# A norm shared by two engines, logits read by token from one bank, and the routing cut short

## The reference, cut to what matters

```python
x = layernorm(target)                      # (32, 256, 128): 32 batches, 256 tokens, 128 features
# branch 1: attention, 16 heads of width 8, causal, then proj, + x, layer norm, * gamma + beta
qkv = x @ w_qkv; scores = q @ k.T / sqrt(8); attn = softmax(causal(scores))
a = layernorm((attn @ v) @ w_proj + b_proj + x) * ln_gamma + ln_beta
# branch 2: mixture of 8 experts, each token goes to its 2 best
probs = softmax(x @ Wr.T); topv, topi = top_k(probs, 2)
m = sum_k topv[k] * (gelu(x @ W1[topi[k]] + b1[topi[k]]) @ W2[topi[k]] + b2[topi[k]])
out = target + a + m
```

## Time and profile before

| | |
|---|---|
| median of 3 runs | 861.58 us (860.87 to 865.58) |
| the profiled execution: time, span | 864.38 us, 862.6 us |
| mean granted TensorE clock | 0.94 of full speed |
| busy share of the span: PE, DVE, ACT, POOL | 82%, 81%, 62%, 62% |
| TensorE clock and PE busy in slices 2 to 5 of 40 (22 to 108 us) | 0.5 to 0.9 of full speed; 3 to 7 tenths |
| the chain that ended last: PE, DVE, DMA | 62%, 13%, 7% |

### The profile page before, as it was taken

One profiled execution on the slowest core, in us unless ns is written; L12 is line 12 of the kernel. 1 busy time (PEld: TensorE's weight loads), 2 busy tenths in 40 slices (PEclk: granted clock), 3 DMA queues, 4 the chain that ended last, 5 costly groups with the idle time before them and its releaser, 6 DMA issues.

```text
span 862.6 us, 24985 instructions
## 1 busy us (share of the span) xinstructions
PE 708.1 (82%) x7699; PEld 523.8 (61%) x7700; DVE 701.1 (81%) x1644; ACT 534.9 (62%) x1061; POOL 533.9 (62%) x572
## 2 busy tenths in 40 slices
PE   0463479999999999999999988857999999999900
PEld 0241246666666666666666556536888898888800
DVE  4866877899989989998989988857888888888745
ACT  0472046565667566666666656537989999999800
POOL 4619046767777776767777677533667776667710
PEclk9985779999999999999999999988999999999955
DMA  7922123232323323232324343111332333323189
GB/s 216 398 59 98 43 65 102 84 113 80 108 89 99 105 80 105 81 110 79 119 86 149 107 125 109 51 33 43 86 85 81 87 87 84 85 79 84 56 260 335
DMA packets 107105, 93.66 MB, mean 109 GB/s; under 512 B 16554, under 2 KB 89394, under 8 KB 107060
## 3 DMA queue, kind: packets, MB, share of 16 engines
q1 hardware_dynamic: 89300, 70.26, 26.2%
q0 software_dynamic: 8704, 18.17, 6.5%
q10 hardware_dynamic: 9056, 4.66, 1.8%
HBM read 43.85 MB, written 48.93 MB: 108 GB/s over the span
## 4 chain that ended last, share of the span: by engine, by line
PE 62%; DVE 13%; DMA 7%; issue 6%; SPq 4%; ACT 2%; POOL 2%; DVEq 1%; POOLq 0%; ACTq 0%
PE wide L1243 11%; PE bank_head L1133 7%; PE bank_head L1234 6%; PE bank_maxB L1234 6%; PE wide L1098 5%; PE bank_maxA L1112 4%; PE bank_maxB L1112 4%; DMA xn_rows<-parts_dram 3%; PE bank_misc L1155 3%; DMA k_cat<-qk_rows 3%; DVE shift L903 2%; PE wide L1102 2%; PE bank_maxA L1116 2%; PE bank_maxB L1116 2%; SPq L458 2%
## 5 line engine op out<-in xcount | busy, mean ns | idle before, releaser
L558 POOL TENSOR_SCALAR_AFFINE_SELECT probs<-probs 128x512 f32<-128x512 f32 (+1 forms) x192 | 155.8, 820 | 102.1 <-ACT probs L648 101.7
L648 ACT ACTIVATE probs<-wide 128x1024 f32<-128x1024 f32 x192 | 188.8, 1018 | 42.4 <-PE wide L1102 22.0
L596 POOL DMA_INDIRECT parts_dram<-o_T,dest x144 | 160.3, 1114 | 74.9 <-issue 47.7
L549 POOL DMA_INDIRECT x_slots<-xn_rows,slot_i x128 | 127.1, 993 | 59.0 <-issue 30.0
L903 DVE TENSOR_REDUCE shift<-bank_maxA 128x2 f32<-128x512 f32 (+1 forms) x192 | 132.1, 688 | 18.9 <-PE bank_maxA L1116 12.5
L903 DVE TENSOR_REDUCE shift<-bank_maxB 128x2 f32<-128x512 f32 (+1 forms) x192 | 131.5, 685 | 4.9 <-PE bank_maxB L1116 0.8
L693 ACT ACTIVATE probs<-wide,b_all 128x256 f32<-128x256 f32 x288 | 121.4, 478 | 17.3 <-PE wide L1243 9.5
L1243 PE MATMUL wide<-lgT,xnT_all 128*128 128x256 f16 x864 | 107.9, 275 | 4.3 <-DVE lgT L1014 4.1
L1133 PE MATMUL bank_head<-probs,v_aug 128*32 128x256 f32 (+1 forms) x2048 | 98.1, 332 | 12.8 <-POOL probs L558 12.3
L997 DVE TENSOR_TENSOR probs<-probs 128x512 f16<-128x512 f32 x144 | 99.7, 693 | 5.5 <-ACT probs L699 1.1
L1112 PE MATMUL bank_maxA<-k_cat,q_diag 128*128 128x128 f16 (+1 forms) x512 | 76.2, 252 | 33.1 <-DVE shift L903 18.9
(11 more groups left out here) (174 smaller groups left out, 1293.3 us busy)
## 6 DMA issues: line engine op xcount, KB each, us to landing
qk_rows<-split SPq DMA_DIRECT2D x32, 512.0 KB, 3.2
x_slots<-fill SPq DMA_DIRECT2D x16, 598.5 KB, 7.1
fill<-x_slots SPq DMA_DIRECT2D x72, 133.0 KB
q_diag<-qk_rows SPq DMA_DIRECT2D x256, 32.0 KB
k_cat<-qk_rows SPq DMA_DIRECT2D x64, 128.0 KB
xn_rows<-parts_dram SPq DMA_DIRECT2D x8, 1024.0 KB, 11.8
out<-x_all ACTq DMA_DIRECT2D x8, 512.0 KB, 9.6
parts_dram<-o_T,dest POOLq DMA_INDIRECT x144
```

Source lines behind the costliest of these rows:

```text
L549: pool.indirect_dma_start(out=x_slots, out_offset=bass.IndirectOffsetOnAxis(ap=slot_i[:, t, c:c + 1], axis=0), in_=xn_rows[:, t, :], in_of ...
L558: pool.affine_select(out=part, in_=part, compare_op=ALU.is_ge, fill=0.0, base=0, pattern=[[0, n], [1, P]], channel_multiplier=-1).then_inc ...
L596: pool.indirect_dma_start(out=parts_dram, out_offset=bass.IndirectOffsetOnAxis(ap=dest[:, of, t:t + 1].bitcast(U32), axis=0), in_=y[:, of ...
L648: act.activation(probs[:, u, :], ps[:, :], ACT.Exp, scale=SCALE).then_inc(empty, 1)
```

## The change

- **Norm.** The input comes in eight half chunks. DVE does all statistics first, then also a small `offset` = -mean * rstd for each chunk; ACT normalises groups 0 to 9 itself, straight from the input (`Identity` with scale and bias, four operations a group), DVE groups 10 to 15. Both write `xn_all` directly; `stage`, `stage_T` and their copies are gone, and so are the loops around these groups. PE transposes from `xn_all`, and ACT makes one copy of each PSUM bank, `xnT_all`.
- **Logits.** PE takes the transposed tile as the stationary operand and the router's weights (8 columns) as the moving one, so that logits come out by token, all 64 tiles in one PSUM bank (`wide[0]`). The transposes back and the copies L615, L619 are gone.
- **Clearing.** `q_diag` is cleared in two halves after the first and second power, `v_aug` after the third.
- **Picks.** They compare logits straight from PSUM, without the exponential; the marks are bf16; PE counts both picks by accumulation. 12 operations. The exponential moves to ACT after step 1, the division and the small weights into `places`.
- **Beta.** POOL adds `beta` for one batch in each step, ahead of the power L585, in place of the eight pieces L544. DVE's `last` waits for it in each step.
- **Experts.** `pack_experts` runs after step 3 in place of step 32; `split_b2` in step 33, after `oT1`.

```diff
+        others, place, rank, prob = (probs[:, u, 0:NT * E].rearrange("p (t e) -> p t e", e=E) for u in range(4))
+        is_top16, key16 = (probs[:, 4, NT * E // 2 * u:NT * E // 2 * (u + 1)].bitcast(BF16).rearrange("p (t e) -> p t e", e=E) for u in range(2))
+        pick16 = probs[:, 5, 0:NT * E].bitcast(BF16).rearrange("p (c t e) -> p c t e", c=2, e=E)
...
+        logits = wide[0][:, 0:NT * E].rearrange("p (t e) -> p t e", e=E)
...
-        ROUTE_PICKED = 18
+        ACT_GROUPS = 10
+        ROUTE_PICKED = 11
         EXPERTS_PACKED = 16
-        ROUTE_DONE = 43
...
+        ROUTE_DONE = 38
+        def wait_normed(eng, g):
+            if g < ACT_GROUPS:
+                eng.wait_ge(normed_act, g + 1)
+            else:
+                eng.wait_ge(normed_dve, g - ACT_GROUPS + 1)
...
-            for c in range(CHUNKS):
...
+            for c in range(2 * CHUNKS):
+                cols = slice(c * TC // 2, (c + 1) * TC // 2)
+                sp.dma_start(x_all[:, cols, :], xt[:, cols, :]).then_inc(x_loaded[c], 16)
...
+            sp.wait_ge(consts, 28)
...
-                    pool.memset(q_diag[:, :, :, :, :], 0.0).then_inc(consts, 1)
-                elif c == 1:
+                if c < 2:
+                    pool.memset(q_diag[:, c, :, :, :], 0.0).then_inc(consts, 1)
+                elif c == 2:
                     pool.memset(v_aug[:, :, :, :, :], 0.0).then_inc(consts, 1)
-                    pool.wait_ge(consts, 26)
+                    pool.wait_ge(consts, 27)
                     pool.memset(v_aug[:, :, :, :, HD:HD + 1], 1.0).then_inc(consts, 1)
...
+            wait_normed(pool, ACT_GROUPS - 1)
+            wait_normed(pool, GROUPS - 1)
...
+                    mine = x_all[:, bass.ds(b * QT, QT), :]
+                    pool.tensor_tensor(mine, mine, beta_bc[:, :].rearrange("p (o d) -> p o d", o=1).to_broadcast([P, QT, D]),
+                                       ALU.add).then_inc(offset_ready, 1)
...
+            def copy_group(g):
                 act.wait_ge(xnT_filled, g + 1)
...
+                act.activation(xnT_all[:, g * (4 * P):(g + 1) * (4 * P)], bank[("maxA", "maxB")[g % 2]][:, :], ACT.Copy).then_inc(xnT_ready, 1)
+            for g in range(GROUPS):
+                if g < ACT_GROUPS:
+                    act.wait_ge(moments_ready, g // (GROUPS // CHUNKS) + 1)
+                    for t in range(4 * g, 4 * g + 4):
+                        ins = act.activation(xn_all[:, t, :], x_all[:, t, :], ACT.Identity, bias=offset[:, t:t + 1], scale=rstd[:, t:t + 1])
+                    ins.then_inc(normed_act, 1)
+                if g > 0:
+                    copy_group(g - 1)
+            copy_group(GROUPS - 1)
             def exp_of_logits():
...
+                act.wait_ge(less_top, 2)
+                act.activation(prob[:, :, :], prob[:, :, :], ACT.Exp).then_inc(exp_router, 1)
+                act.activation(top[:, 1, :], top[:, 1, :], ACT.Exp).then_inc(exp_router, 1)
...
+            def normalise_group(g):
+                for t in range(4 * g, 4 * g + 4):
+                    ins = V.tensor_scalar(xn_all[:, t, :], x_all[:, t, :], mean[:, t:t + 1], rstd[:, t:t + 1], ALU.subtract, ALU.mult)
+                ins.then_inc(normed_dve, 1)
+            def offsets(c):
+                cols = slice(c * TC, (c + 1) * TC)
+                dve.wait_ge(rstd_ready, c + 1)
+                V.scalar_tensor_tensor(out=offset[:, cols], in0=mean[:, cols], scalar=-1.0, in1=rstd[:, cols],
+                                       op0=ALU.mult, op1=ALU.mult).then_inc(moments_ready, 1)
             count = 2
...
+            for c in range(CHUNKS):
+                for h in range(2):
+                    dve.wait_ge(x_loaded[2 * c + h], 16)
+                    for t in range(c * TC + h * TC // 2, c * TC + (h + 1) * TC // 2):
+                        V.bn_stats(stats[:, t, :], x_all[:, t, :]).then_inc(prep, 1)
...
+                if c > 0:
+                    offsets(c - 1)
+            offsets(CHUNKS - 1)
+            for g in range(ACT_GROUPS, GROUPS):
+                normalise_group(g)
...
+                then(V.tensor_copy(order16[:, :], order[:, :]))
+                dve.wait_ge(logits_filled, 1)
+                for c in range(2):
+                    of = (logits, others)[c]
+                    then(V.tensor_reduce(top[:, c, :], of[:, :, :], axis=AX.X, op=ALU.max))
+                    then(V.tensor_tensor(is_top16[:, :, :], of[:, :, :], over_experts(top[:, c, :]), ALU.is_equal))
+                    then(V.tensor_tensor(key16[:, :, :], is_top16[:, :, :], over_tiles(order16[:, :], NT), ALU.mult))
+                    then(V.tensor_reduce(best[:, c, :], key16[:, :, :], axis=AX.X, op=ALU.max))
+                    then(V.tensor_tensor(pick16[:, c, :, :], over_tiles(order16[:, :], NT), over_experts(best[:, c, :]), ALU.is_equal))
                     if c == 0:
...
+                        then(V.scalar_tensor_tensor(out=others[:, :, :].rearrange("p t e -> p (t e)"),
+                                                    in0=pick16[:, 0, :, :].rearrange("p t e -> p (t e)"), scalar=-FAR,
+                                                    in1=wide[0][:, 0:NT * E], op0=ALU.mult, op1=ALU.add))
+                assert route_count == ROUTE_PICKED + 1, route_count
             def places():
                 nonlocal route_count
...
+                V.tensor_tensor(prob[:, :, :], logits[:, :, :], over_experts(top[:, 0, :]), ALU.subtract).then_inc(less_top, 1)
+                V.tensor_tensor(top[:, 1, :], top[:, 1, :], top[:, 0, :], ALU.subtract).then_inc(less_top, 1)
+                then(V.tensor_scalar(xn_rows[:, :, D + 4], best[:, 0, :], -1.0, float(E), ALU.mult, ALU.add))
                 dve.wait_ge(route_counts, 1)
...
+                total = wide[1][:, 512:1024]
+                then(V.tensor_reduce(padded[:, :], total.rearrange("p (t e) -> p e t", e=E), axis=AX.X, op=ALU.add))
+                then(V.tensor_scalar(padded_i[:, :], padded[:, :], float(S - 1), None, ALU.add))
                 then(V.tensor_scalar(padded_i[:, :], padded_i[:, :], S.bit_length() - 1, None, ALU.logical_shift_right))
                 then(V.tensor_scalar(padded[:, :], padded_i[:, :], float(S), None, ALU.mult))
                 then(V.tensor_tensor_scan(ends[:, :], ones[:, 0:E], padded[:, :], 0.0, ALU.mult, ALU.add))
                 then(V.tensor_tensor(padded[:, :], ends[:, :], padded[:, :], ALU.subtract))
...
+                for e in range(E):
+                    V.tensor_tensor_scan(place[:, :, e], ones[:, :], total.rearrange("p (t e) -> p t e", e=E)[:, :, e],
+                                         padded[:, e:e + 1], ALU.mult, ALU.add).then_inc(route, 1)
+                    route_count += 1
+                dve.wait_ge(exp_router, 2)
+                then(V.tensor_reduce(red[:, :], prob[:, :, :], axis=AX.X, op=ALU.add))
+                then(V.tensor_tensor(rank[:, :, :], wide[1][:, 0:512].rearrange("p (t e) -> p t e", e=E), place[:, :, :], ALU.add))
                 for c in range(2):
...
+                    V.tensor_tensor((others, place)[c][:, :, :], pick16[:, c, :, :], rank[:, :, :], ALU.mult).then_inc(route, 1)
+                    route_count += 1
+                then(V.reciprocal(xn_rows[:, :, D], red[:, :]))
+                then(V.tensor_tensor(red[:, :], top[:, 1, :], xn_rows[:, :, D], ALU.mult))
+                then(V.tensor_tensor(xn_rows[:, :, D + 2], red[:, :], xn_rows[:, :, D], ALU.subtract))
+                for c in range(2):
+                    V.tensor_reduce(slot[:, c, :], (others, place)[c][:, :, :], axis=AX.X, op=ALU.add).then_inc(route, 1)
+                    route_count += 1
+                for c in range(2):
+                    dve.wait_ge(route, route_count - 1)
                     then(V.tensor_copy(slot_i[:, :, c], slot[:, c, :]))
...
+                        if what == "oT1" and isinstance(s, int) and s == B + 1:
+                            split_b2()
...
-                if isinstance(s, int) and s == B:
-                    split_b2()
+                if isinstance(s, int) and s == FINISH:
                     pack_experts()
...
+            def router(g):
+                pe.wait_ge(xnT_ready, g + 1)
+                for t in range(4 * g, 4 * g + 4):
+                    last = M(logits[:, t, :], xnT_all[:, P * t:P * (t + 1)], wrT[:, 0:E], start=True, stop=True, skip_group_check=True)
+                if g == GROUPS - 1:
+                    last.then_inc(logits_filled, 1)
...
+            for g in range(GROUPS):
+                wait_normed(pe, g)
+                if g > 1:
+                    pe.wait_ge(xnT_ready, g - 1)
+                ps = bank[("maxA", "maxB")[g % 2]]
...
+                pe.wait_ge(route, ROUTE_PICKED + 1)
+                for n_, counting in enumerate((after16, ones16)):
+                    for c in range(2):
+                        last = M(wide[1][:, 512 * n_:512 * (n_ + 1)], counting[:, :], pick16[:, c, :, :].rearrange("p t e -> p (t e)"),
```

(15 more changed lines are left out.)

178 lines of the change are left out of this document (24 added, 154 removed).

## The result

The changed kernel takes 851.98 us (median of 4, 850.38 to 853.92) where the kernel before takes 861.46 beside it: ratio 0.9868, 95% interval 0.9834 to 0.9903. A second set gave 0.9882 (0.9852 to 0.9911). It is faster by 1.2 to 1.3%; forecast were 3.3%, and the range (825 to 848) did not hold the time. The profiled execution took 853.92 us, and its span is 852.2 us against 862.6.

A forecast was written before the change was run, and what follows sets the result against it. PE paces the pipeline; time can come from prologue, routing and behind step 32, where PE waits. Terms -20.5 - 9.5 + 0.5 + 1.5 + 3.7 - 3.9 = -28.2 us: 864.4 to 836.2 profiled, 833.5 median; range 825 to 848.

The forecast's parts named there:

- PE's line in the prologue: Prologue, TensorE: 1.3 us a group at the higher clock, six last groups from 38.7 to 46.5, then first projection at 48.
- low-clock rival: Prologue: PE's clock stays low, first projection at 56, kernel 841.5 us; chance 0.17.
- my 48: End of prologue: first projection starts at 48 instead of 68.46, a gain of 20.5 us, bounds 12.5 to 23.
- Statistics and powers: Prologue, DVE and POOL: first chunk landed at 10.93, power 0 at about 13.8, last offset at 37.4.
- my upper case: Prologue, ACT: if activations don't overlap, 0.38 each, a group takes 2.1 us and ten groups end near 42.
- a running memset: Prologue: `mean` waits for POOL's running clearing, so each power behind a memset starts some 0.5 us late.
- Picks: Routing behind the first projection: 12 operations, L919 10.9 us after the first instead of 20.4; gain 9.5 us.
- Places: Routing behind the picks: more count products, other small operations; 10.0 us becomes 10.4 to 10.6, cost 0.5 us.
- Beta: POOL's add in each step: 0.05 us a step, cost 1.5 us in all, bounds 0 and 21.8.
- loop rival: Pipeline steps: beta's add delays L937 and the maxima by its own length each step, 21.8 us, kernel 854; chance 0.10.
- Pack: Packing after step 3 costs 3.7 us (bounds 3.5 to 5.5); its absence behind step 32 gains 3.9 us.
- the 0.3 in the pack's: Behind step 32: 0.3 us allowed for a semaphore and the slower clock, in the 3.9 us gain there.

## Why the prediction was wrong

**The step that failed** is PE's line in the prologue: "a group needs 4 loads for transposes and 8 for the router [...] so 1.3 or 2.1; the moving side of 8 columns hides behind the loads", and "at the higher level the six last groups take PE from 38.7 to 46.5". Three things in it were wrong. I took the higher level, 1.3 us a group, and the longer durations stood throughout, for which the same count gives 2.1. The products were not wholly hidden either: a group is 2.46, between the 2.1 and the 2.8 that I had written down as the bound for products not hidden. And I started the count at group 10, as if PE had caught up with ScalarE by 38. With 2.46 us a group against 1.64 + 0.48 on ScalarE it falls behind from the second group on. Behind 22.31 lie fifteen sets of transposes and sixteen of router products: 22.3 + 0.95 x 15 + 1.51 x 16 is 60.7; measured 60.98. The low-clock rival (56) had the right engine and the right level, but the same error in the start.

That PE's work for the router is what holds this prologue is shown by the router experiments: with three of four products left out the projection starts at 46.67, with each made twice at 88.22, with the old operands at 51.33 and 47.37. They do not separate the order of the operands from the clock level. An estimate: if the changed order's products shrank as the transposes (1.12 to 0.66) and the old order's products (0.66 to 0.43) do, a group would be about 1.5 us, below ScalarE's 2.0, and PE would not have been the bound in spite of the order. No run had these products at the shorter durations, so whether the changed order can reach them stays open. That 46.67 is near my 48 does not confirm my 1.3 a group: PE there has two router passes a group for eight, mostly at the longer durations.

**Statistics and powers** came earlier than I wrote: the first power at 10.91 instead of 13.8, as VectorE found both halves of the first chunk there and took its sixteen statistics from 6.44 on without a wait, where I had put the chunk's landing at 10.93; and the last offset at 34.03 instead of 37.4. **ScalarE** needs 0.41 for each 128x128 activation from SBUF in a row (1.64 for four), not the 0.25 of the earlier trace rows; that is my upper case (2.1 a group), and it did not matter behind PE. What I took of a running memset held: `mean` (now L764) took 2.32 and 2.75 us beside the two halves of `q_diag`'s clearing, for 5.79 before.

**Picks** were right: 9.5 forecast, 10.1 measured, and L901 of step 1 starts 10.5 behind the first operation on logits (10.9 forecast; 64.70 and 75.23). Of the bf16 pairs only one kind got cheap: L801, marks times the order along the inner dimension, 0.42, for 0.69 of L803, whose one operand repeats one value along it. By the Trainium skill (VectorE: DVE Perf Modes, Mode 2×_1P) two elements a cycle want a step of one element in memory; the two rows agree, and the saving of 0.27 in each of two is what the prediction estimated. VectorE had 1.39 us left at the end:

```profile
64.70 0.69 DVE L799 TENSOR_REDUCE top<-wide 128x64 f32<-128x512 f32 x1
...
66.15 0.42 DVE L801 TENSOR_TENSOR probs<-probs,order 128x512 bf16<-128x512 bf16 x1
...
67.33 0.69 DVE L803 TENSOR_TENSOR probs<-order,best 128x512 bf16<-128x512 bf16 x1
...
72.55 0.69 DVE L885 TENSOR_REDUCE shift<-bank_maxA 128x4 f32<-128x512 f32 x1 [0.46 <-PE bank_maxA L1080]
...
75.23 0.69 DVE L901 TENSOR_TENSOR split<-bank_misc,split 128x512 f16<-128x512 f32 x1 [1.39 <-ACT split L658]
```

**Places** took 10.7 (82.69 to 93.39; forecast 10.4 to 10.6). Steps 1 to 3 around it gained 1.9 that I had not counted.

**Beta** at 1.5 for all steps can't be called right or wrong: 0.26 is read in the length of three steps, and the rest is below what a ratio tells. The loop rival (21.8 us) did not happen; L919 keeps 0.17 to 0.18 there, and from the end of step 4 to that of step 23 both kernels take 265.8 us. The mechanism of that rival is seen in the written-out steps only, by the 0.26 above. The 4.4 us between the ends of steps 23 and 32 have in them 2.4 of step 26 (the wait for `k_cat` and the longer durations behind it), 0.8 of beta and 1.4 of step 32. Step 32 takes 14.94 us where PE waits 1.50 for `k_cat` in it (14.99 and 1.54 without beta), and 13.53 and 13.38 in the kernel before and that with beta in pieces, where it does not. Against that step 29 gives back 1.1. Without beta 2.7 are lost there all the same, and in the second profile of the changed kernel 1.8.

**Pack** early was mis-sized: 5.4 and not 3.7. Its 16 operations took 4.9 in a chain; what the hole of 0.99 in step 4 gave back went into new waits for a PE that the gap had slowed down. The sum had no price for that. Its gain in the tail was 5.5 (forecast 3.9), then 3.4 were lost in step 34.

**The tail's clock** had no term but the 0.3 in the pack's: I had looked for it only in front of the pipeline. The earlier trace rows has 0.52 behind step 32 in the kernel before, so the place was known to be one where PE idles and the clock drops.

By the leads the miss of 17.8 us is: prologue 13.0; from there to the end of step 3 -2.3; early pack 1.7; steps 4 to 32 3.0; tail 2.4.

**What stays open:** why the granted clock falls behind the same gap in one execution and not in another; whether the changed order of the router's operands can run at the shorter durations; and why PE waits for `k_cat` in one step of one profile and not of another. Between 420 and 550 these waits are 2.7 us in three places in the kernel before, 4.1 in three and 2.0 in two in the two profiles of the changed kernel, and 5.2 in four without beta. They go some way to explain the 2 to 3 us that steps 24 to 32 lose even without beta, but no run here took them away alone.

## What to carry to other kernels

When an f32 product has one long and one short operand, count what each order makes the engine load: with the 8-column side moving the router took 1.72 us a group, with the weights stationary 0.66 at the same level and 0.43 at the higher one, which outweighed the helper operations that this order needs. When a stage is split over several engines, add up every engine from the stage's first item and not from where the others finish; the one that is slowest per item has fallen behind long before. A chain of small dependent instructions can be cut up and dealt out between long instructions of its engine: by the lengths of the steps the pack cost 1.8 us so, against 5.4 and 3.3 in one piece, though the medians of the last two places can't be told apart.

## What the runs showed of the hardware that was not expected

A router product with 128 stationary and 8 moving columns costs as much as its loads. Timeline of PE's load side in the changed kernel, two groups of sixteen passes in all:

```profile
57.35 3.54 PEld L1027 LDWEIGHTS wide<-wrT,xnT_all 128*128 128x128 f32 x16
```

That is 0.22 a pass; at 71.41 four f16 loads of the same 128x128 (L1076) take 0.34, 0.085 each. By the Trainium skill (TensorE: Matmul & The Clock Gate, Weight-path perf modes) the fast weight load is for 128 columns of a type other than f32; that the f32 ones are 2.6 times as long agrees. Two dense f16 products a group made neither these nor the transposes shorter. The column of the granted clock shows 1.00 in that whole stretch, and 0.81 to 0.94 in stretches of the kernel with the old operands where four transposes take 0.66: in the prologue the durations, not the column, tell at which level the engine runs. In the tail column and durations agree (0.64 and 2.74 us for twelve products, 0.94 and 1.49), and the two levels came in two executions whose instructions on PE had stood at the same places, within 0.1 us, for the 20 us before.
